# A decoder kernel on one core: the row maxima go back before the next batch's big load

## What is computed

```python
q = einsum('oc,bct->bot', Wq, target) + bq      # target: layer-normed x
k = einsum('oc,bcs->bos', Wk, source) + bk      # source: ctx
v = einsum('oc,bcs->bos', Wv, source) + bv
# 16 heads of 8 dimensions, T = S = 256
dot = einsum('bhdt,bhds->bhts', q, k) / sqrt(8)
dot = mask * dot - (1 - mask) * 1e6
amap = softmax(dot, axis=-1) * mask
out = einsum('bhts,bhds->bhdt', amap, v)
x = x + tanh(g) * out
```

## Time and profile before

| what | value |
|---|---|
| runs | 553.83, 559.36, 560.20 us; median 559.36 |
| profiled execution | 558.33 us, its span 556.5 us |
| PE busy | 483.7 us, 87% of the span |
| DVE busy | 379.6 us, 68% |
| ACT busy | 247.5 us, 44% |
| POOL busy | 229.2 us, 41% |
| mean granted TensorE clock | 0.972 |
| SP's DMA queue | 55.24 MB, 36.9% of the time of 16 DMA engines |

### The profile page before, as it was taken

One profiled execution on the slowest core, in us unless ns is written; L12 is line 12 of the kernel. 1 busy time (PEld: TensorE's weight loads), 2 busy tenths in 40 slices (PEclk: granted clock), 3 DMA queues, 4 the chain that ended last, 5 costly groups with the idle time before them and its releaser, 6 DMA issues. The chain is left out here.

```text
span 556.5 us, 10469 instructions
## 1 busy us (share of the span) xinstructions
PE 483.7 (87%) x3384; PEld 264.7 (48%) x3384; DVE 379.6 (68%) x768; ACT 247.5 (44%) x478; POOL 229.2 (41%) x303
## 2 busy tenths in 40 slices
PE   2859999998898788988898989787979989899994
PEld 2634564745533433333333433332434545688873
DVE  4986879788589777788788888795757433333331
ACT  2732233121232177878788888677711100133321
POOL 2753224142367165666555565412110730024424
PEclk9987999999999979999999999899999999999998
DMA  7747600000175525555556665510050241168753
GB/s 214 214 145 166 104 1 0 1 1 2 57 195 143 130 57 150 147 143 143 141 141 147 162 156 135 146 28 5 1 157 1 91 165 47 58 167 185 196 127 38
DMA packets 67254, 59.94 MB, mean 108 GB/s; under 512 B 10048, under 2 KB 62256, under 8 KB 67216
## 3 DMA queue, kind: packets, MB, share of 16 engines
q1 hardware_dynamic: 63424, 55.24, 36.9%
q0 software_dynamic: 3072, 4.21, 4.4%
q10 hardware_dynamic: 720, 0.00, 0.1%
HBM read 38.90 MB, written 22.50 MB: 110 GB/s over the span
## 5 line engine op out<-in xcount | busy, mean ns | idle before, releaser
L1175 DVE TENSOR_REDUCE MX<-psum 128x2 f32<-128x512 f32 x256 | 161.3, 683 | 34.4 <-PE psum L1054 33.4
L1215 ACT ACTIVATE HP<-psum 128x512 f32<-128x512 f32 x256 | 137.5, 598 | 56.4 <-PE psum L1068 55.4
L1054 PE MATMUL psum<-QKA 60*128 60x256 bf16 x512 | 83.7, 281 | 13.8 <-DVE MX L1175 10.1
L1068 PE MATMUL psum<-QKA 60*128 60x256 bf16 x512 | 79.4, 281 | 16.1 <-DMA QKA<-max_scr 12.6
L1141 PE MATMUL psum<-HP,VP 128*32 128x256 f32 x1024 | 84.0, 402 | 0.2 <-ACT HP L1215 0.2
L512 PE MATMUL psum<-space_a,space_w 128*128 128x512 f32 x160 | 75.0, 618 | 1.1 <-ACT space_a L497 0.8
L1054 PEld LDWEIGHTS psum<-QKA 60*128 60x128 bf16 x512 | 35.9, 96 | 69.3 <-DVE MX L1175 47.9
L1736 POOL DMA_INDIRECT out_x<-OE,to_u x16 | 25.0, 1564 | 75.7 <-ACT OE L1777 73.2
L512 PEld LDWEIGHTS psum<-space_a,space_w 128*128 128x128 f32 x160 | 30.3, 197 | 37.9 <-issue 35.3
L525 ACT ACTIVATE space_a<-psum,hgs 128x512 f32<-128x512 f32 (+1 forms) x24 | 15.6, 651 | 70.3 <-PE psum L512 47.8
L1875 PE MATMUL psum<-XT,WE 128*128 128x256 f32 (+1 forms) x192 | 44.3, 380 | 2.4 <-ACT XT L1761 1.6
(11 more groups left out here) (186 smaller groups left out, 735.3 us busy)
## 6 DMA issues: line engine op xcount, KB each, us to landing
QKA<-stack_scr SPq DMA_DIRECT2D x32, 480.0 KB, 5.4
stack_scr<-PARTS SPq DMA_DIRECT2D x32, 192.0 KB, 2.0
WE<-in_W SPq DMA_DIRECT2D x16, 352.0 KB
stack_scr<-PARTS SPq DMA_DIRECT2D x32, 128.0 KB, 1.9
XD<-dispatched SPq DMA_DIRECT2D x8, 258.0 KB, 3.7
X<-in_x SPq DMA_DIRECT2D x4, 512.0 KB, 5.6
CTX<-in_ctx SPq DMA_DIRECT2D x4, 512.0 KB, 8.2
MB<-in_mask SPq DMA_DIRECT2D x16, 128.0 KB, 5.7
```

The source lines that it names most:

```text
L1054: return pe.matmul(to[:, tt * T:(tt + 1) * T], QKA[rows, k, 0, h, tt * P:(tt + 1) * P], QKA[rows, k, 1, h, :], start=True, stop=True)
L1068: return pe.matmul(to[:, (m % 2) * T:(m % 2 + 1) * T], QKA[rows, k, 1, h, st * P:(st + 1) * P], QKA[rows, k, 0, h, :], start=True, stop=True)
L1175: dve.tensor_reduce(MX[:, par, head_of(n), :], src[:, :].rearrange("p (a s) -> p a s", a=2), axis=AX.X, op=ALU.max).then_inc(a_red, 1)
L1215: act.activation(PT[:, i % 2, st, 2 * half:2 * half + 2, :].rearrange("p j t -> p (j t)"), TBK3[THIRDS[m]], ACT.Exp).then_inc(a_exp, 1)
```

## The change

- `sp_batch`: the fill of b + 3 moves from first place to behind the maxima's load of b + 1.
- PE: `pe_mxT` moves from the end of slot 0 into slot 1, behind that slot's `pe_pv`, and now waits for `act_qk` of b + 4, which ACT does in slot 0. The projection of b + 5 moves from slot 6 to slot 7.
- ACT: `act_nm` moves from slot 0 to slot 1, behind AV and two exponentials; `act_qk` from slot 7 (b + 5) to the next turn's slot 0 (b + 4).
- Ramp: the queries of batches 2 and 4 are projected in bank 7 and at other places; PE's wait for both of DVE's additions before turn 0 becomes a wait for one bank at a time; the last group's statistics are spread over turns 0 to 2 instead of standing before turn 0; POOL's power step of that group moves to turn 2.

```diff
@@ sp_batch
                             b = GB * g + k
-                            if there(b, 3):
-                                sp_fill(sp, *at(g, k, 3))
                             if there(b, 1):
                                 sp_max_store(sp, *at(g, k, 1))
...
                             if there(b, 1):
                                 sp_max_fill(sp, *at(g, k, 1))
+                            if there(b, 3):
+                                sp_fill(sp, *at(g, k, 3))
                             if there(b, 4):
                                 sp_store(sp, *at(g, k, 4))
@@ ACT, slot
-                            if p == 0 and there(b, 1):
+                            if p == 0 and not first(b) and there(b, AHEAD_Q):
+                                act_qk(act, b + AHEAD_Q)
+                            if p == 1 and there(b, 1):
                                 act_nm(act, b + 1)
-                            if p == 2 and first(b):
-                                act_qk(act, AHEAD_Q)
-                            if p == 7 and there(b, AHEAD_Z):
-                                act_qk(act, b + AHEAD_Z)
@@ PE, slot
                             if p == 1 and there(b, -1):
                                 pe_pv(pe, *at(g, k, -1), 3, st)
+                            if p == 1 and there(b, 1):
+                                if there(b, AHEAD_Q):
+                                    pe.wait_ge(a_qk, b + AHEAD_Q + 1)
+                                else:
+                                    pe.wait_ge(a_x3, b - 1)
+                                pe_mxT(pe, *at(g, k, 1))
...
-                            if p == 0 and there(b, 1):
...
-                                pe_mxT(pe, *at(g, k, 1))
-                            if p == 1 and first(b):
-                                pe.wait_ge(a_nm, 2)
-                                pe_proj_q(pe, *at(g, k, AHEAD_Q))
-                            if p == 6 and there(b, AHEAD_Z):
...
+                            if p == 7 and there(b, AHEAD_Z):
+                                if first(b):
+                                    pe.wait_ge(a_nm, 2)
+                                else:
+                                    pe.wait_ge(a_x3, b)
+                                pe_proj_q(pe, *at(g, k, AHEAD_Z))
@@ PE, ramp
                         if last:
-                            pe.wait_ge(a_qk, 1)
-                            pe_proj_q(pe, 0, 2, QB[0])
                             pe_gu(pe, G3, 0)
+                            pe.wait_ge(s_x2, 1 + 2 * G3)
+                            pe_proj_q(pe, 0, 2)
...
-                            if (b, p) == (0, 0):
-                                pe.wait_ge(a_qk, AHEAD_V)
                             pe_scores(pe, 0, b, p, PRO)
...
+                            if (b, p) == (1, 4):
+                                pe.wait_ge(a_nm, 1)
+                                pe_proj_q(pe, 1, 0)
...
-                        pe.wait_ge(s_x2, 1 + 2 * NG)
@@ pe_both
+                        if first(GB * to_turn[0] + to_turn[1]) and p == 0:
+                            pe.wait_ge(s_x2, 1 + 2 * G3 + n + 1)
@@ DVE
+                        dve_z3(dve, AHEAD_Q)
                         reduces(1, 0, 16)
                         dve_x2(dve, G3, DB)
-                        dve_stats3(dve, ln3, G3)
...
+                            if isinstance(b, int) and 8 * b + p in LAST_STATS:
+                                dve_one_of_last(dve, ln3, LAST_STATS.index(8 * b + p))
```

More of the change, by code:

```diff
@@ L211, in flamingo_kernel @@
             NS = GB
+            G3 = NG - 1
             HALF = HEADS // 2
@@ L662, in dve_stats3, with dve_one_of_last @@
                    .then_inc(a_var, 1)
+            def dve_one_of_last(dve, ch, i):
+                if i < GB:
+                    ch.do(dve.bn_stats(stats3[:, i, :], X[:, GB * G3 + i, :]))
+                    return
+                ch.wait()
+                alone(dve)
+                for t in range(GB):
+                    ch.do(dve.bn_aggr(mv3[:, GB * G3 + t, :], stats3[:, t, :]))
+                ch.wait()
+                dve.tensor_scalar(veps3[:, GB * G3:B], mv3[:, GB * G3:B, 1], EPS, None, ALU.add).then_inc(a_var, 1)
             def pool_power3(pool, g):
@@ L669, in flamingo_kernel @@
             QB = [bank[4], bank[5]]
-            G3 = NG - 1
             N_CHAIN, N_SMALL, N_ROWS = 5, 9, 14
@@ L1161, in pool_z3 @@
                 def pool_z3(pool, pch, b):
-                    pool.wait_ge(a_rstd, NG)
+                    pool.wait_ge(a_rstd, b // GB + 1 if isinstance(b, int) else NG)
                     pool.wait_ge(a_proj, b)
@@ L1329, in flamingo_kernel @@
                 LN4, TURN4 = 3, 9
+                LAST_STATS = [2, 4, 10, 12, 18]
                 with nc.Block() as block:
@@ L1377, in _ @@
                             if i == 2:
-                                act_qk(act, 2, QB[0])
+                                act_qk(act, 2)
                             if i == 3:
@@ L1386, in _ @@
                         act_part(act, AHEAD_V, 1)
+                        act_qk(act, AHEAD_Q)
                         act.wait_ge(s_dn, 1 + 2 * NG)
@@ L1428, in _ @@
                         pool_vp(pool, pch, 0, 2)
-                        pool_power3(pool, G3)
                         def slot(pch, g, k, p):
@@ L1434, in slot @@
                                 pool_power4(pool, tail(b, p) - LN4)
-                            if p == 0 and not first(b) and there(b, AHEAD_Q):
+                            if p == 0 and there(b, AHEAD_Q):
                                 pool_masked(pool, *at(g, k, AHEAD_Q))
@@ L1438, in slot @@
                                 pool_np(pool, pch, b + 1)
-                            if p == 2 and first(b):
-                                pool_masked(pool, *at(g, k, AHEAD_Q))
+                            if p == 3 and isinstance(b, int) and b == 2:
+                                pool_power3(pool, G3)
                             if p == 4 and there(b, AHEAD_Z):
@@ L1471, in _ @@
                                     pair()
-                            if i == 1:
+                            if i == 3:
+                                pe.wait_ge(a_qk, AHEAD_V)
                                 pe_proj_q(pe, 0, AHEAD_V)
@@ L1554, in slot @@
                                 dve_reduce(dve, *at(g, k, AHEAD_S), 2 * p)
-                            if p == 1 and first(b):
-                                dve_z3(dve, AHEAD_Q)
                             if there(b, AHEAD_S):
                                 dve_reduce(dve, *at(g, k, AHEAD_S), 2 * p + 1)
+                            if isinstance(b, int) and 8 * b + p in LAST_STATS:
+                                dve_one_of_last(dve, ln3, LAST_STATS.index(8 * b + p))
                             if p == 3 and there(b, -1):
```

## The result

The changed kernel takes 597.88 us (median of 4 runs, 595.87 to 598.68), the kernel before 559.09 us beside it: ratio 1.071, 95% interval 1.064 to 1.078. The forecast was 599, range 574 to 612. The profiled execution took 595.87 us, its span is 594.1. In the changed kernel the plain scores stand at L1066 and the transposed ones at L1080.

The account below looks back on a forecast made before the run. No resource was full; SP's closed round of 12.85 us bound turns 0 to 12. Moving the fill makes a serial round of 16.8 us a turn: 558.3 + 42.3 - 1.2 (ramp) = 599 us, range 574 to 612.

Parts of the forecast that it names:

- The step that decided: Turns 0 to 12: fill landing, maxima's chain and next fill run without overlap, 16.8 us a turn, +42.3 us in all.
- The forecast's 0.2 us: Start of each turn on PE: from fill landed to first transposed score, 0.1 for one score matmul and 0.1 of reaction.
- first matmul to NM: PE and ACT: NM comes 3.9 us after the first transposed score, with bias, AV and two exponentials ahead of it.
- POOL's split: POOL: from NM to the end of the split of the maxima, 2.3 us.
- issue, landing, reaction of the maxima's store: SP: issue 0.1, landing 2.7, reaction 0.1 us; 2.7 taken because a mask load is issued behind the store.
- fill issued to next first matmul: The fill's pair of DMAs is complete 6.6 us after the first issue; the next turn's first matmul waits for it.
- a case in which PE's clock falls in each wait: Rival on PE: clock falls to the 1.2 GHz level, adding 0.3 to 1.0 us a turn, 603 to 611 us; chance 0.15.
- The rival of quicker transfers: Store lands in 1.5 us, fill in 6.3, giving 14.8 us a turn, 13.6 for turn 0, 573 us; chance 0.20.
- Turn 0: First attention turn, with neither AV nor a bias ahead of NM: NM at 2.7 us, the turn 15.6 us.
- What the profile was to show: Fill to fill 16 to 17.5 us, store landing 1.5 to 3, 12 or 13 PE fill waits of 3 to 5, lower DMA share.
- The ramp: Before and in the first turns: shorter PE waits, less batch 4's projection at +0.6; together -1.2 us, between -2.5 and +0.5.
- The diagnosis behind the change: SP's queue: the fill ahead of the maxima's store costs the maxima 3.3 to 4.5 us each turn.

Follow-up runs that it names:

- Experiments 1 to 4: Changed kernel with fill first: 555.91 us; kernel before with fill behind: 564.60; changed kernel with old slots, fill first: 556.17; the same with fill behind: 563.75.
- experiment 9: Changed kernel with 18 more transposes on PE at the head of each turn from 1 on, ahead of its wait for the fill: 583.22 us.
- experiment 3: Changed kernel with the fill first and PE's and ACT's slots as before, leaving only the new ramp and spread statistics: 556.17 us.
- experiments 2 and 4: Fill behind the maxima's load with old slots: in the kernel before, old ramp, 564.60 us; in the changed kernel, new ramp, 563.75 us.
- experiments 6 and 8: Kernel before with the fill between the maxima's store and their load: 546.50 us; the same with the new ramp: 542.60 us.
- experiment 6: Kernel before with the fill between the maxima's store and their load, old slots and old ramp: 546.50 us.
- experiment 7: Changed kernel, with its new slots and ramp, but the fill between the maxima's store and their load: 574.74 us.

## Why the prediction was right

**The step that decided was right.** It was that the moved fill has a second end: from the turn's first matmul to the fill's landing all is serial, and its length is the turn's. Twelve turns of 16.8 us forecast, 16.55 measured; turns 0 to 12 together 217.2 forecast, 212.7 measured. Experiments 1 to 4 show the mechanism: either move alone is within 1% of before, both together are 7% slower.

**Its terms were less right than their sum.** The forecast's 0.2 us is split in two, 0.1 on either side of the first matmul. Forecast against the turn at 252.67:

| term | forecast | measured |
|---|---|---|
| first matmul to NM | 4.0 | 4.75 |
| POOL's split | 2.3 | 2.30 |
| issue, landing, reaction of the maxima's store | 2.9 | 1.66 |
| load issued to fill issued | 0.9 | 1.00 |
| fill issued to next first matmul | 6.7 | 7.26 |

The term of the store was mis-sized by 1.2 us, because I took the one row of 2.7 us over the one of 1.5 us and gave the mask load behind it as the reason; the changed kernel has a mask load behind 11 of its 16 stores, and 10 of those landed in 1.5 us, one in 1.8, the other five in 1.4 to 1.5. So the reason was wrong. What held up the store of 196.84 stays open. The Trainium skill's 2.0 us of fixed cost (DMA: Bandwidth & Descriptors, Anatomy of one DMA, for the path that GpSimd issues) is above what this trace shows for SP's small store. The store's error was made good by two terms on the other side: 0.75 us up to NM, and 0.6 us for the fill, which varies. This turn is 0.4 us longer than the mean of the twelve, in which it is 4.7 us from the first matmul to NM (4.0 forecast), 4.9 from there to the fill (6.1) and 6.9 from the fill to the next first matmul (6.7).

**The clock was not a rival but a part.** I gave 0.15 to a case in which PE's clock falls in each wait and put it at +4 to +12 us beside the sum. It did fall, in 11 of the turns 1 to 12 (mean granted clock 0.86 over turns 0 to 12, 190.5 to 403.2, against 0.95 in the earlier trace rows), and experiment 9 measures it at 14.7 us. The pattern is the one that the Trainium skill describes (TensorE: Matmul & The Clock Gate, HAM oscillation), a loop whose DMA waits each cost the clock. With the store at 1.5 us and no fall of the clock, my sum is 15.6 a turn, and experiment 9 has 15.71. So two errors, the store's (1.2 us in each of 13 turns, some 15 us) and the clock's (14.7 us), cancelled in the forecast of 599. That it came within 2 us of the median is luck; that the round is closed and sets the turn is not. The rival of quicker transfers had the store right. Its own terms add up to 14.9 a turn and 13.9 for turn 0, not the 14.8 and 13.6 that it names, which makes it 575 us, and it left out the clock.

**Turn 0** took 14.1 us, not 15.6: nearly all of the difference is the store's term again.

**What the profile was to show** came out but for one point. Fill to fill, the landing of the store and the lower DMA share (0.46 against 0.53 in the earlier trace rows) are as forecast, but PE's waits for the fill in turns 1 to 13 are 1.6 to 3.4 us long, not 3 to 5. The forecast took the work of a turn as 11.9 us; at the lower clock the same matmuls took longer (PE is busy 163.7 us in turns 0 to 12, where it was 152.6). The next maxima's store, forecast some 5 us after the fill's landing, came 7.15 us after the turn's first matmul.

**The ramp** brought turn 0 forward by 1.1 us, as forecast (1.2). By itself it is worth 4 us in experiment 3. That comes, as far as SP's timeline tells, from the earlier projection of batch 4, of which I had priced only PE's 0.6 us. Where the fill is behind, the ramp gives about 1 us (564.60 and 563.75 in experiments 2 and 4, no difference beyond their intervals): in the changed kernel batch 4's parts are stored from 199.98, and its fill leaves at 213.76, behind the maxima.

**The diagnosis behind the change** was right, as forecast: the fill ahead cost the maxima 4.5 us (6.0 to 1.5). Half the remedy, the store ahead and the fill directly after it, gives 2.4% by itself.

## What to carry to other kernels

A transfer that is moved behind another to give way waits for everything which that one waits for; before it is moved, look up who needs its landing, and add the chain from the start of the loop's body to that landing. If it comes out near the length of the body, only the part that must go ahead should go ahead (here a store of 24 KB, behind which the fill could leave 0.5 to 1.1 us later), not the round trip behind it. Two moves of which each is harmless can close a loop together, so slots that feed a transfer and the transfer's own place are to be judged as one.

## What the runs showed of the hardware

- In the changed kernel a wait of 2.8 us on TensorE cost more than itself: the granted clock was 1.00 in the wait, 0.55 from 253 to 254 and 0.50 (1.2 GHz) from 254 to 256, after work had begun again at 252.67. The 16 `pe_pv` matmuls at 253.51 took 1.93 us instead of 1.07, and `pe_mxT` 0.40 instead of 0.28. 18 transposes in the wait, 2.13 us of work that nobody reads, kept the clock at 1.00 and made the kernel 14.7 us faster.
- A store of 24 KB to DRAM landed in 1.5 us in 10 of 11 cases with a mask load of 128 KB issued 0.4 to 1.0 us behind it (changed kernel), and in 24 of 26 with the fill, 960 KB, issued 0.5 to 1.1 us behind it (experiments 6 and 8); with 960 KB ahead of it on the same queue it took 5.7 to 7.1 us (kernel before). Single stores took 1.7 to 2.9 us; one of 2.8, at 371.85 in experiment 6, had nothing issued behind it before it landed. Their cause is open.
- The later of the fill's two DMAs of 480 KB landed 6.0 to 6.7 us after its issue in the changed kernel, but 7.6 us once in experiment 7 and 7.5 us once in experiment 6. The latter left right behind a maxima's store that also landed late (2.9 us). What delayed them was not looked into.
